# Second adjacency product, written out by step: three raw weight buffers, halves made one or two steps ahead, weights turned two steps later

## The chip, the cores and the metric

One core of a Trainium2 chip runs the whole program. The metric is the device time of one execution in microseconds, the median of several runs. TensorE is called PE here, VectorE DVE, ScalarE ACT, GpSimd POOL, SyncE SP.

## The reference, cut to what matters

Inputs: x (2048 x 512), adj (2048 x 2048), the weights of one shared and eight routed experts, a router, gamma and beta. All is float32.

```python
S = adj + adj.T, plus the identity, scaled on both sides by 1/sqrt(degree)
x = x + (adj @ S) @ layernorm(x)
h = layernorm(layernorm(x)) * gamma + beta
# _bit_quant: each row of a weight matrix becomes -1, 0 or +1 times the row's mean of abs
shared = silu(h @ q(w1s).T) @ q(w2s).T
routed = top-1 of 8 experts: gate * silu(h @ q(w1e).T) @ q(w2e).T
out = x + shared + routed
```

The kernel computes the graph term as two products: z = S u (first adjacency product), then y = adj z (second adjacency product). The change is about the second one and the work that runs beside it.

## The kernel before

**Stages.** To about 100 us adj and its transpose are streamed in and the first product is begun; to 198 us the first product is finished for the other columns while 28 weight chunks are quantised ("early rounds"). From 198 to 391 us the second product runs, 48 steps of it, with 36 more weight chunks beside it. From 391 us on the feed-forward tiles run, first the shared expert's, with the last 8 chunks beside them, then the routed ones.

**One step of the second product** (`macro` on each engine, four steps to a macro; J counts steps from 0 to 47). The 2048 output rows are done in groups of 6, 6 and 4 tiles of 128 rows (`Y_GROUPS`), each with its own PSUM banks `acc[k]` and 16 steps, one for each 128 rows of adj_t. In a step SP loads a strip of adj_t (`load_at`, 128 x 768 or 128 x 512 float32, two buffers, three in the last group), ACT makes its high float16 half (`high`, L924), DVE the low half (`low`, L1331), and PE does three matmuls of 512 columns for each bank: high by high, high by low, low by high (`parts`, L1622 to L1624). A step has 18 matmuls in the first two groups and 12 in the last. There are two buffers of halves, three in the last group.

**One weight chunk** (128 x 1024, q counts them; chunk 28 is the first of this stage; one a step except in steps 32 to 35 and from step 40 on). SP loads it (`load_w`, L489 and L492, two raw buffers), ACT sums its absolute values (`sums`, L871), DVE scales it to a byte (`ternary`, L1232 to L1259), PE transposes four blocks (`turn_w`, L1652), and ACT takes the sign back into SBUF (`store_w`, L885) three steps after its sums. Before PE turns chunk q, chunk q-2 must have been stored (`wt_ok`). Some early chunks are turned by a DMA on SP's queue (`turn`, L469), among them 25 and 27, and stored by L881.

**Between the groups** DVE adds x to the finished banks (`x1_of_group`, L1359), ACT issues the stores of these rows (`store_x1`, L961), and rows already there are normalised in pairs of tiles: part one and part two on DVE (`norm_parts`, L1303 to L1309 and L1314 to L1318), between them a power on POOL (L718), afterwards the halves of h on ACT (`h_high`, L955) and POOL (L725), and their store by POOL (L729). ACT waits for the stores of group 0 at step 20 and of group 1 at step 36 (`x1_stored`), before anything else of that step.

Each engine takes its instructions in the written order; across engines only semaphores order them. In a step ACT's order is high of J, store of chunk J-3, sums of chunk J, h_high; DVE's is low of J, ternary of J, normalising; PE's is turning the chunk of the step before, then the matmuls of J. On SP the load of adj_t for J comes before the load of the weights for J, and the first waits until the low half of J-2 has been made.

```python
pe.wait_ge(wt_ok, q - 1)                 # turn_w: chunk q-2 has been stored
pe.wait_ge(atlo_ok, STEPS * m + s + 1)   # macro on PE: the low half of this step
dve.wait_ge(p2_step, NT * (g + 1))       # x1_of_group: all banks of the group are done
```

## Time and profile before

| | us |
|---|---|
| median of 3 runs (669.05 to 671.61) | 669.19 |
| the profiled execution, its own time | 671.48 |
| its span, first to last instruction | 669.9 |
| PE busy | 616.7 (92%) |
| DVE busy | 481.1 (72%) |
| ACT busy | 373.1 (56%) |
| POOL busy | 179.0 (27%) |
| second product, first to last matmul | 198.2 to 391.1 |

Busy PE time is modelled for the end of each matmul; records of neighbours overlap, so the step from one start to the next says more than the duration. A "q" behind an engine's name is its sequencer: it issues DMAs and counts as no busy time. Idle time in square brackets stands before the instruction, with what ended it.

### The profile page before, as it was taken

The page shows a single profiled execution, that of the slowest core. Times are in us where ns is not written, and L with a number is a line of the kernel's source. Part 1 is how long each engine was busy: PE and PEld are TensorE (multiplying, and loading weights), DVE is VectorE, ACT ScalarE, POOL GpSimd, SP SyncE. Part 2 cuts the span into 40 slices and gives each one's busy share as a digit, 9 for nine tenths or more (in the row PEclk, how much of TensorE's full clock was granted, in tenths as well). Part 3 has the DMA queues.
Part 4 walks back from the last instruction along what each step waited for, and adds up shares of the span by engine and source line. Part 5 has one row for each costly group of instructions (what it writes and reads, how often), then busy time and mean ns, then how long its engine had stood idle before and what let it go on. Part 6 is the DMA issues. An engine that isn't in the chain of part 4 may idle for free.

```text
span 669.9 us, 14592 instructions
## 1 busy us (share of the span) xinstructions
PE 616.7 (92%) x4713; PEld 348.7 (52%) x4713; DVE 481.1 (72%) x1075; ACT 373.1 (56%) x699; POOL 179.0 (27%) x208
## 2 busy tenths in 40 slices
PE   0789899999999899999988999999999999999994
PEld 0334344444443444444433467776766676676762
DVE  4878986777775555677888659877885567666664
ACT  1667756677986777678756423556643334333241
POOL 2234343222210000003222406100120454444432
PEclk9999999999999899999999999999999999999999
DMA  8999990895878778777767966987249587788742
GB/s 341 417 417 416 421 356 15 175 239 160 233 206 282 241 256 290 267 250 230 233 226 246 226 184 140 242 208 200 80 67 235 152 198 184 173 167 194 182 135 59
DMA packets 106655, 149.81 MB, mean 224 GB/s; under 512 B 64510, under 2 KB 64510, under 8 KB 102496
## 3 DMA queue, kind: packets, MB, share of 16 engines
q1 hardware_dynamic: 91280, 116.82, 58.6%
q0 software_dynamic: 6512, 20.07, 10.3%
q10 hardware_dynamic: 8800, 12.09, 6.1%
q8 instruction: 38, 0.62, 0.4%
q14 instruction: 25, 0.20, 0.1%
HBM read 117.73 MB, written 18.25 MB: 203 GB/s over the span
## 4 chain that ended last, share of the span: by engine, by line
PE 47%; issue 29%; DVE 10%; DMA 8%; POOL 3%; ACT 1%; POOLq 0%; DVEq 0%; SPq 0%; ACTq 0%
PE bank L1745 14%; PE bank L1773 13%; DMA region<-in_adj_t 6%; PE bank L1622 5%; PE bank L1624 5%; PE bank L1623 5%; PE bank L1788 2%; DVE region L1145 2%; PE bank L1802 1%; DMA hb<-h_scratch,zreg 1%; DVE region L1141 1%; POOL rb L718 1%; DVE work L1400 1%; POOL hb L725 1%; DMA work<-hb 1%
## 5 line engine op out<-in xcount | busy, mean ns | idle before, releaser
L1773 PE MATMUL bank<-region,work 128*128 128x512 f16 (+1 forms) x512 | 116.9, 379 | 3.7 <-DVE work L1410 3.4
L1622 PE MATMUL bank<-zreg,work 128*128 (+1 forms) x256 | 97.7, 382 | 10.6 <-DVE work L1331 7.8
L1001 ACT ACTIVATE work<-work 128x512 f32<-128x512 f32 x64 | 39.8, 621 | 106.5 <-DVE work L1400 106.5
L1622 PE MATMUL bank<-region,work 128*128 128x512 f16 x192 | 74.0, 386 | 26.1 <-DVE region L1169 26.1
L1623 PE MATMUL bank<-zreg,work 128*128 (+1 forms) x256 | 97.5, 381 | 0.0
L1624 PE MATMUL bank<-zreg,work 128*128 (+1 forms) x256 | 97.5, 381 | 0.0
L871 ACT ACTIVATE junk<-work 128x512 f16<-128x512 f32 x116 | 72.8, 627 | 26.9 <-DMA work<-in_w 19.4
L1773 PEld LDWEIGHTS bank<-region,work 128*128 128x128 f16 x512 | 46.6, 98 | 61.6 <-issue 9.1
L1745 PE MATMUL bank<-zreg,region 128*128 128x128 f16 x1280 | 75.7, 219 | 0.0
L1745 PEld LDWEIGHTS bank<-zreg,region 128*128 128x128 f16 (+1 forms) x1280 | 72.7, 98 | 3.7
L1623 PE MATMUL bank<-region,work 128*128 128x512 f16 x192 | 74.0, 385 | 0.0
L1624 PE MATMUL bank<-region,work 128*128 128x512 f16 x192 | 73.8, 384 | 0.0
L1410 DVE SCALAR_TENSOR_TENSOR work<-work 128x512 f16<-128x512 f32 x64 | 43.6, 689 | 29.3 <-ACT work L1008 28.3
L1400 DVE TENSOR_TENSOR work<-bank,s 128x512 f32<-128x512 f32 x64 | 41.2, 685 | 25.7 <-PE bank L1745 24.6
L924 ACT ACTIVATE work<-work 128x768 f16<-128x768 f32 (+1 forms) x46 | 35.2, 764 | 38.9 <-PE bank L1624 21.2
L1259 DVE TENSOR_SCALAR work<-work,thr 128x512 int8<-128x512 f32 (+1 forms) x82 | 49.5, 634 | 4.1
L1331 DVE SCALAR_TENSOR_TENSOR work<-work 128x768 f16<-128x768 f32 (+1 forms) x48 | 42.6, 892 | 11.1 <-ACT work L924 10.9
L885 ACT ACTIVATE region<-bank 128x1024 f16<-128x1024 int8 (+1 forms) x44 | 44.3, 1007 | 6.8 <-DVE region L1359 6.8
L1745 PE MATMUL bank<-work,region 128*128 128x128 f16 x768 | 46.4, 220 | 1.1 <-DMA work<-hb 1.1
L1622 PEld LDWEIGHTS bank<-zreg,work 128*128 128x128 f16 x256 | 25.1, 98 | 41.4 <-DVE work L1331 8.5
L1745 PEld LDWEIGHTS bank<-work,region 128*128 (+1 forms) x768 | 43.6, 98 | 4.6 <-issue 2.0
L1622 PEld LDWEIGHTS bank<-region,work 128*128 128x128 f16 x192 | 19.0, 99 | 51.7 <-issue 20.7
(198 smaller groups left out, 1010.8 us busy)
## 6 DMA issues: line engine op xcount, KB each, us to landing
work<-in_w SPq DMA_DIRECT2D x58, 512.0 KB, 4.2
region<-in_adj SPq DMA_DIRECT2D x16, 1024.0 KB, 10.7
region<-in_adj_t SPq DMA_DIRECT2D x16, 1024.0 KB, 7.5
work<-in_adj_t SPq DMA_DIRECT2D x32, 384.0 KB, 4.4
xb<-in_w SPq DMA_DIRECT2D x10, 512.0 KB, 4.2
zreg<-s_scratch SPq DMA_DIRECT2D x17, 256.0 KB, 3.9
zreg<-in_x SPq DMA_DIRECT2D x4, 1024.0 KB, 9.8
h_scratch<-hb POOLq DMA_DIRECT2D x16, 256.0 KB, 4.4
```

Of the source, the lines that this page charges most:

```text
L871: nc.scalar.activation(junk[:, :], src[:, a * D:(a + 1) * D], ACT.Abs, accum_out=asum[:, b, a:a + 1]).then_inc(abs_ok, 1)
L885: nc.scalar.activation(values, pst8[turn_bank(q, b)], ACT.Sign).then_inc(wt_ok, 1)
L1001: nc.scalar.activation(h1[:, cols], pre[:, cols], ACT.Silu).then_inc(h1_ok, 1)
L1259: ins = nc.vector.tensor_scalar(bytes_, rows, thr[:, b, 0, a:a + 1], None, ALU.mult)
L1331: nc.vector.scalar_tensor_tensor(out=dst[:, 1, :], in0=src, scalar=A_SCALE, in1=dst[:, 0, :], op0=ALU.mult, op1=ALU.subtract).then_inc(atl ...
L1400: nc.vector.tensor_tensor(pre[:, half * 512:(half + 1) * 512].rearrange("p (f t) -> p f t", f=4), ps_h[b][half][:, :].rearrange("p (f t) - ...
L1410: nc.vector.scalar_tensor_tensor(out=h1hl[:, b, 1, cols], in0=h1[:, cols], scalar=U_SCALE, in1=h1hl[:, b, 0, cols], op0=ALU.mult, op1=ALU. ...
L1622: nc.tensor.matmul(dst, a_hi, b_hi, start=start, stop=False, skip_group_check=True)
L1623: nc.tensor.matmul(dst, a_hi, b_lo, start=False, stop=False, skip_group_check=True)
L1624: return nc.tensor.matmul(dst, a_lo, b_hi, start=False, stop=False, skip_group_check=True)
L1745: last = nc.tensor.matmul(ps_h[b][f // 4][:, (f % 4) * P:(f % 4 + 1) * P], w, ht[n % RING][:, c:c + P], start=(f % 4 == 0 and d == 0 and h ...
L1773: last = nc.tensor.matmul(ps_y[b][:, :].rearrange("p (d c) -> p d c", d=DB), h1hl[:, b, h, f * P:(f + 1) * P], w, start=(f == 0 and h == 0 ...
```

## The change

The stage is written out for all 48 steps instead of in loops of four, and its order is changed:

- Raw weights have three buffers instead of two. The load of chunk q waits for the quantising of chunk q-3 instead of q-2, and stands one step earlier in SP's queue.
- Halves have three buffers (four in the last group). In step J ACT and DVE make the halves of step J+1, in the last group those of J+2.
- PE turns the chunk of step J-2 in step J, instead of that of J-1.
- In the last step of a group each bank counts `y_acc`, and DVE evicts it singly, instead of all once the step is over. In step 32 DVE evicts four banks, makes a low half, and evicts the other two.
- The stores of the scales (`store_s2`) and of the rows of the first two groups (`store_x1`) move from ACT's queue to POOL's; those of group 1 stand there behind the third pair of tiles (t = 4) and ahead of the fourth (t = 6).
- The evictions that finish z (`z_high(2)`, `z_low(2)`) stand before the last early chunk instead of behind it.

The functions that go are in the listing above; here is the core of what comes.

```diff
--- before.py
+++ after.py
...
+RAW_RING = 3
...
         raw = work[:, 6144:6144 + 4096].bitcast(F32).rearrange("p (b n) -> p b n", b=2)
+        raw_more = w2t[:, 8 * CHUNK:10 * CHUNK].bitcast(F32)
+        hl_more = w2t[:, 10 * CHUNK:11 * CHUNK]
+        low_more = w2t[:, 7 * CHUNK:7 * CHUNK + HL]
...
+        def chunk_of(J):
+            if 0 <= J < 2 * NT:
+                return J
+            i = J - STEPS
+            return i if 2 * NT <= i < LATE_FROM - EARLY_CHUNKS else None
+        def raw_at(i):
+            return raw[:, i % RAW_RING, :] if i % RAW_RING < 2 else raw_more
+        def at_tile(J):
+            return at_end[:, J % NT % 3, :] if J >= 2 * NT else at[:, J % 2, 0:HL]
+        def at_landed(J):
+            if J >= 2 * NT:
+                return at_end_loaded[J % NT % 3], 16 * (J % NT // 3) + 16
+            return at_loaded[J % 2], 16 * (J // 2) + 16
+        def at_read(J):
+            if J >= 2 * NT + 3:
+                return J - 2
+            return min(J, 2 * NT + 1) - 1 if J <= 2 * NT else 2 * NT
+        def halves_at(J):
+            if J >= 2 * NT:
+                r = (J % NT + 3) % 4
+                return [hl_end[:, r, h, :] if r < 3 else hl_more[:, h * MH:(h + 1) * MH] for h in range(2)]
+            r = J % 3
+            return [hl[:, r, 0, :], hl[:, r, 1, :]] if r < 2 else [hl_more[:, 0:HL], low_more[:, :]]
+        def steps_before_halves(J):
+            k = J - 2 * NT
+            if k >= 4:
+                return J - 3
+            return (2 * NT - 2, 2 * NT - 1, 2 * NT, 2 * NT)[k] if k >= 0 else J - 2
+        def ahead_at(J):
+            if J < 2 * NT:
+                return [J + 1] if J >= 2 else [2] if J == 0 else []
+            return [n for n in ((J + 1, J + 2) if J == 2 * NT else (J + 2,)) if n < 3 * NT]
...
+            def load_w(i):
+                q, kind, c = later(i)
+                sp.wait_ge(tern_ok, q - 2)
+                if i == 2:
+                    sp.wait_ge(z_acc, NT)
...
+            def load_at(J):
+                g, j = divmod(J, NT)
+                c0, nc_ = Y_GROUPS[g][0] * P, Y_GROUPS[g][1] * P
+                if J >= 2:
+                    sp.wait_ge(atlo_ok, at_read(J))
+                sp.dma_start(at_tile(J), adjt_j[j, :, c0:c0 + nc_]).then_inc(at_landed(J)[0], 16)
...
+            load_w(0)
+            def y_step(J):
+                if chunk_of(J + 1) is not None:
+                    load_w(chunk_of(J + 1))
+                if J + 2 < 3 * NT:
+                    load_at(J + 2)
+                if J < 2:
+                    turn(EARLY_CHUNKS - 3 + 2 * J)
+                if J < NT and J % STEPS == STEPS - 1:
+                    t = 3 * (J // STEPS)
+                    if t == 0:
                         sp.wait_ge(z_acc, NT)
-                    sp.dma_start(xg_r[:, ds(3 * m, 3), :], x_t[:, ds(3 * m, 3), :]).then_inc(xg_in, 16)
+                    sp.dma_start(xg_r[:, t:t + 3, :], x_t[:, t:t + 3, :]).then_inc(xg_in, 16)
+                if J in (2 * NT + 9, 2 * NT + 10):
+                    load_last_x(J - 2 * NT - 9)
+                elif 2 * NT + 11 <= J <= 2 * NT + 14:
+                    load_shared(J - 2 * NT - 11)
...
+            def store_x1(g):
+                t0, count = Y_GROUPS[g]
+                for k in range(t0, t0 + count, 2):
+                    pool_wait(x1_ok, k + 2)
+                    pool.dma_start(x1_t[:, k:k + 2, :], xg_r[:, k:k + 2, :]).then_inc(x1_stored, 16)
+            store_s2(0, EARLY0, CHUNKS, S2_FROM[0])
+            store_s2(1, 0, 4, S2_FROM[1])
+            store_x1(0)
...
-            with pool.Fori(0, Y_GROUPS[2][0] // 2) as i:
+            with pool.Fori(0, Y_GROUPS[1][0] // 2) as i:
+                norm_pair(2 * i, pair=i)
+            store_x1(1)
+            with pool.Fori(Y_GROUPS[1][0] // 2, Y_GROUPS[2][0] // 2) as i:
                 norm_pair(2 * i, pair=i)
             norm_pair(12, True)
...
+                    if q == EARLY_CHUNKS - 1:
+                        z_high(2)
...
+            def high(J):
+                act.wait_ge(*at_landed(J))
+                if J >= 3:
+                    act.wait_ge(p2_step, steps_before_halves(J))
+                nc.scalar.activation(halves_at(J)[0], at_tile(J), ACT.Copy, scale=A_SCALE).then_inc(athi_ok, 1)
+            def y_step(J, norm_t=None):
+                for n in ahead_at(J):
+                    high(n)
+                if J == 1:
+                    store_w(early_at(EARLY_CHUNKS - 2), EARLY_CHUNKS % 2)
+                elif J == 3:
+                    store_w(early_at(EARLY_CHUNKS - 1), (EARLY_CHUNKS - 1) % 2)
+                i = chunk_of(J - LAG)
+                if i is not None:
+                    store_w(later(i), i % 2)
+                i = chunk_of(J)
+                if i is not None:
+                    act.wait_ge(raw_loaded[i % RAW_RING], 16 * (i // RAW_RING) + 16)
+                    sums(later(i), i % 2, raw_at(i))
+                if norm_t is not None:
+                    for e in range(2):
+                        h_high(norm_t + e, e)
...
-            z_high(2)
             store_w(early(ROUNDS - 1, early_count(ROUNDS - 1) - LAG), (EARLY_CHUNKS - LAG) % 2)
...
+            H_STEPS = {6 * STEPS: 0, 7 * STEPS: 2, 8 * STEPS: 4, 9 * STEPS + 1: 6, 10 * STEPS + 1: 8, 11 * STEPS + 1: 10}
+            for J in range(3 * NT):
+                if J == 5 * STEPS:
+                    act.wait_ge(x1_stored, 48)
+                elif J == 9 * STEPS:
+                    act.wait_ge(x1_stored, 96)
+                y_step(J, H_STEPS.get(J))
...
-                    if rnd == ROUNDS - 1 and s >= ROUND_STEPS - 2:
-                        low(0, s - ROUND_STEPS + 2, s % 2)
+                    if rnd == ROUNDS - 1 and s == ROUND_STEPS - 2:
+                        low(0)
+                    elif rnd == ROUNDS - 1 and s == ROUND_STEPS - 1:
+                        z_low(2, (0, 1))
+                        low(1)
+                        z_low(2, (2, 3))
...
+            NORM_STEPS = {STEPS * m + p * (1 if m == 7 else 2): (p, 2 * m - 10)
+                          for m in range(5, MACROS - 1) for p in range(2)}
+            def y_step(J):
+                ahead = ahead_at(J)
+                if J == NT:
+                    low(ahead[0])
+                    x1_of_group(0, xg_r[:, 0:6, :], range(6))
+                elif J == 2 * NT:
+                    low(ahead[0])
+                    x1_of_group(1, xg_r[:, 6:12, :], range(4))
+                    low(ahead[1])
+                    x1_of_group(1, xg_r[:, 6:12, :], range(4, 6))
+                else:
+                    for n in ahead:
+                        low(n)
+                i = chunk_of(J)
+                if i is not None:
+                    ternary(later(i), i % 2, raw_at(i))
+                if J in NORM_STEPS:
+                    norm_parts(*NORM_STEPS[J])
...
-                dve.wait_ge(p2_step, NT * (g + 1))
-                for k in range(count):
+                for k in ks:
+                    if k < count - 1:
+                        dve.wait_ge(y_acc, (Y_GROUPS[0][1] - 1) * g + k + 1)
+                    else:
+                        dve.wait_ge(p2_step, NT * (g + 1))
...
+            def y_step(J):
+                g, j = divmod(J, NT)
+                i = chunk_of(J - 2)
+                if i is not None:
+                    turn_w(later(i), i)
+                pe.wait_ge(atlo_ok, J + 1)
+                for k in (2, 3, 4, 5, 0, 1) if J == 0 else range(count):
+                    if J == 0:
+                        pe.wait_ge(zlo_ok, Z_LAST[k])
+                    elif j == 0:
+                        pe.wait_ge(x1_ok, Y_GROUPS[g - 1][0] + k + 1)
+                    last = parts(acc[k], *[v[:, k * P:(k + 1) * P] for v in halves_at(J)], z_hi[:, j, :], z_lo[:, j, :], j == 0)
+                    if j == NT - 1 and k < count - 1:
+                        last.then_inc(y_acc, 1)
+                last.then_inc(p2_step, 1)
+            for J in range(3 * NT):
+                y_step(J)
```

Where the order moves, by engine. First SP's queue at the start of the stage (work<-in_w are raw weights, work<-in_adj_t strips of adj_t; the transposes are chunks 25 and 27). Before, from the last early load on:

```order
L483 DMA xb<-in_w 128x1024
L469 DMA_TRANSPOSE region<-work 128x4x128
L489 DMA work<-in_w 128x2x512
L469 DMA_TRANSPOSE region<-work 128x4x128
L489 DMA work<-in_w 128x2x512
L497 DMA work<-in_adj_t 128x768
L489 DMA work<-in_w 128x2x512
L497 DMA work<-in_adj_t 128x768
L492 DMA work<-in_w 128x1024
L530 DMA region<-in_x 128x3x512
```

With the change:

```order
L533 DMA xb<-in_w 128x1024
L541 DMA work<-in_w 128x2x512 x2
L552 DMA work<-in_adj_t 128x768
L519 DMA_TRANSPOSE region<-work 128x4x128
L541 DMA region<-in_w 128x2x512
L552 DMA work<-in_adj_t 128x768
L519 DMA_TRANSPOSE region<-work 128x4x128
L544 DMA work<-in_w 128x1024
L552 DMA work<-in_adj_t 128x768
```

The transposes of chunks 25 and 27 stood ahead of the weights of steps 0 and 1; now they stand behind two and three loads.

ACT over the same place (L860 and L929 evict z; L871 and L940 sum; L881, L885 and L950, L954 store a chunk; L924 and L987 make high halves). Before:

```order
L871 ACTIVATE junk,asum<-work 128x512 x2
L885 ACTIVATE region<-bank 128x1024
L871 ACTIVATE junk,asum<-xb 128x512 x2
L860 ACTIVATE zreg<-bank,dinvz 128x512 x4
L881 ACTIVATE region<-region 128x1024
L871 ACTIVATE junk,asum<-work 128x512 x2
L885 ACTIVATE region<-bank 128x1024
L871 ACTIVATE junk,asum<-work 128x512 x2
L924 ACTIVATE work<-work 128x768
L881 ACTIVATE region<-region 128x1024
```

With the change:

```order
L940 ACTIVATE junk,asum<-work 128x512 x2
L929 ACTIVATE zreg<-bank,dinvz 128x512 x4
L954 ACTIVATE region<-bank 128x1024
L940 ACTIVATE junk,asum<-xb 128x512 x2
L950 ACTIVATE region<-region 128x1024
L987 ACTIVATE region<-work 128x768
L940 ACTIVATE junk,asum<-work 128x512 x2
L954 ACTIVATE region<-bank 128x1024
L940 ACTIVATE junk,asum<-work 128x512 x2
L987 ACTIVATE work<-work 128x768
L940 ACTIVATE junk,asum<-region 128x512 x2
L987 ACTIVATE work<-work 128x768
```

z is evicted one chunk earlier. The store of chunk 25 (the first L950 behind the evictions) stands ahead of the first high half, and the store of chunk 27 (the last L950) behind the high half of step 4.

POOL around the end of the third pair of tiles (rb<-rb,power is the power between the two parts of the normalising, h_scratch<-hb the stores of h). Before, one loop over all six pairs:

```order
L732 UNCONDITIONAL_BRANCH
L732 ISA
L718 TENSOR_TENSOR rb<-rb,power 128x2
L724 ISA
L725 TENSOR_TENSOR hb<-xb,hb 128x512
L724 REGISTER_ALU
L725 TENSOR_TENSOR hb<-xb,hb 128x512
L729 ISA
L729 DMA h_scratch<-hb 128x1024
L729 ISA
L729 DMA h_scratch<-hb 128x1024
L732 REGISTER_ALU
```

With the change:

```order
L795 DMA h_scratch<-hb 128x1024
L795 ISA
L795 DMA h_scratch<-hb 128x1024
L798 REGISTER_ALU
L798 COMPARE_AND_BRANCH
L774 DMA x_scratch<-region 128x2x512 x3
L801 UNCONDITIONAL_BRANCH
L801 ISA
L784 TENSOR_TENSOR rb<-rb,power 128x2
L790 ISA
```

The three stores of group 1 (x_scratch) stand behind the third pair and ahead of the power of the fourth, where no other engine's queue held them back before. The stores of scales and of group 0 stand ahead of the first pair in the same way.

## Rows read from the trace of the kernel before

**Rows 1.** PE's waits by window; waiter, awaited, us in total, times, longest; 196 to 268

```profile
PE bank L1652 <- ACT region L885: 2.8, 1, 2.8
PE bank L1622 <- DVE zreg L1219: 1.2, 1, 1.2
PE bank L1652 <- DVE work L1259: 1.1, 1, 1.1
```

**Rows 2.** the same view, 268 to 343.5

```profile
PE bank L1622 <- DVE work L1331: 2.2, 4, 0.8
PE bank L1622 <- DVE region L1359: 1.4, 2, 0.7
```

**Rows 3.** the same view, 343.5 to 391

```profile
PE bank L1622 <- DVE work L1331: 5.6, 6, 1.5
```

**Rows 4.** timeline of PE: start, us, what [idle before]; step 3 and the turn after it

```profile
213.41 0.38 PE L1622 MATMUL bank<-zreg,work 128*128 128x512 f16 x1
...
217.08 0.38 PE L1624 MATMUL bank<-zreg,work 128*128 128x512 f16 x1
220.28 0.61 PE L1652 MATMUL bank<-ident,work 128*128 128x128 f16 x4 [2.81 <-ACT region L885]
```

**Rows 5.** stages: stretch, us, PE busy (count), granted clock, DMA share, GB/s

```profile
220.00:223.00 3.00, 2.73 (x10) 0.50 0.49 126
```

**Rows 6.** timeline of ACT at the start of the stage

```profile
198.56 2.40 ACT L860 ACTIVATE zreg<-bank,dinvz 128x512 f16<-128x512 f32 x4
...
218.47 0.84 ACT L924 ACTIVATE work<-work 128x768 f16<-128x768 f32 x1 [5.05 <-PE bank L1624]
```

**Rows 7.** timeline of SP's queue at the start of the stage

```profile
197.89 0.38 SPq L489 DMA_DIRECT2D work<-in_w  x1
```

**Rows 8.** landing of SP's DMA transposes (L469)

```profile
DMA to landing us min/median/max: 2.4/3.0/5.0
```

**Rows 9.** landing of the strips of adj_t (L497), 195 to 340

```profile
DMA to landing us min/median/max: 2.5/4.3/7.0
```

**Rows 10.** landing of the stores of x1 (L961)

```profile
DMA to landing us min/median/max: 2.8/3.5/5.6
```

**Rows 11.** timeline of ACT around step 32 and later

```profile
342.45 2.76 ACTq L961 DMA_DIRECT2D x_scratch<-region  x3
...
350.45 0.63 ACT L924 ACTIVATE work<-work 128x512 f16<-128x512 f32 x1 [2.21 <-DMA x_scratch<-region]
...
364.81 0.63 ACT L871 ACTIVATE junk<-work 128x512 f16<-128x512 f32 x1 [2.79 <-DMA work<-in_w]
...
366.19 0.61 ACT L924 ACTIVATE work<-work 128x512 f16<-128x512 f32 x1
366.71 1.00 ACT L885 ACTIVATE region<-bank 128x1024 f16<-128x1024 int8 x1
```

**Rows 12.** timeline of DVE, from the eviction of group 1 on

```profile
341.13 3.68 DVE L1359 SCALAR_TENSOR_TENSOR region<-bank,region 128x512 f32<-128x512 f32 x6 [1.58 <-PE bank L1624]
...
345.33 1.27 DVE L1303 BATCH_NORM_STATS2 stb<-region 128x6 f32<-128x512 f32 x2
...
347.05 0.68 DVE L1331 SCALAR_TENSOR_TENSOR work<-work 128x512 f16<-128x512 f32 x1
...
361.15 0.16 DVE L1236 TENSOR_SCALAR s<-asum 128x2 f32<-128x2 f32 x1
...
362.41 1.41 DVE L1314 SCALAR_TENSOR_TENSOR xb<-region,mvb,gb 128x512 f32<-128x512 f32 x2
...
365.06 0.68 DVE L1331 SCALAR_TENSOR_TENSOR work<-work 128x512 f16<-128x512 f32 x1
```

**Rows 13.** timeline of POOL, 339 to 348

```profile
339.32 2.37 POOL L725 TENSOR_TENSOR hb<-xb,hb 128x512 f16<-128x512 f32 x2 [10.31 <-ACT hb L955]
341.63 0.58 POOL L729 DMA_DIRECT2D h_scratch<-hb  x1
...
347.23 1.08 POOL L718 TENSOR_TENSOR rb<-rb,power 128x2 f32<-128x2 f32 x1 [4.27 <-DVE rb L1309]
```

228 lines of the change are left out of this document (48 added, 180 removed).

## Prediction

> **What bounds the kernel now.** The engine shares come first: PE is busy for 92% of the span, so the end moves by what PE gains or loses. Then the waits of PE alone, by stretches of the stage that is changed. At its start PE idles 5.1 us in three waits [rows 1]: for the evicted z, for a quantised chunk, and for 2.8 us for a chunk that ACT had not stored. In the middle, up to the eviction of group 1, it idles 3.6 us in six waits [rows 2], in the last group 5.6 us in six [rows 3]. The timeline of one step shows what a wait really costs: 17 starts take 217.08 - 213.41 = 3.67 us, so 0.216 us each; the next start was due at 217.30 and came at 220.28 [rows 4]. That is 2.98 us for an idle time of 2.81, because the record of a matmul is 0.16 longer than its pitch. So each wait costs its idle time and 0.16. Behind the long one the granted clock is 0.50 (1.2 GHz instead of 2.4) in a stretch of 3 us [rows 5]: 2.7 us of busy time at half speed, 1.35 us lost. In all: start 5.1 + 0.5 + 1.35 = 7.0, middle 3.6 + 1.0 = 4.6, last group 5.6 + 1.0 = 6.6; together **18.2 us**. More this change can't get: matmuls and transposes stay the same in number. Behind the stage everything starts from its last matmul, so I carry its gain to the end one to one.
>
> **Start of the stage.** Evicting z one chunk earlier lets ACT begin at about 196.3 instead of 198.56 [rows 6], and the wait for z shrinks from 1.4 us to some 0.2. But the queues behind it get worse. Two weights have to be stored before PE may turn chunks 28 and 29, and both come late:
>
> - Chunk 28. The transpose of chunk 25 now stands behind the load of weights that is free at 197.89 [rows 7] and a strip of adj_t, with an issue of 0.4 us each: it goes at 198.7. Transposes landed after 2.4 to 5.0 us [rows 8]; I take 4.4, near the upper end, because 896 KB go ahead of it in its queue: 203.1. ACT then stores chunk 25 (1.00), makes the high half of step 2 (0.84) and sums chunk 28 (366.19 - 364.81 = 1.38), and DVE quantises it (362.41 - 361.15 = 1.26) [rows 6, 11, 12]: 207.6, with hand-overs 207.8. PE gets there after two steps of 18 x 0.216 from 198.2, at 206.2 with its turns. It waits 1.6 us (0 with the fastest landing, 2.2 with the slowest).
> - Chunk 29. Its turn asks for chunk 27 to be stored, and on ACT that stands behind the high half of step 4, whose strip stands on SP behind a load that waits until chunk 28 is quantised. From there 0.4 + 4.3 (2.5 to 7.0) [rows 9] + 0.84 + 1.00 = 6.5 us, while PE has 4.1 us of work. It waits 2.4 us (0.6 to 5.1).
>
> The clock may fall again: after idles of 1.2 and 1.1 us it didn't, after 2.8 it did. The second wait is nearest to the latter, so I take one fall, 1.35 us (none to two for the range). The wait on ACT for the stores of the scales (L969), behind which ACT idled 5.05 us and then stood ahead of PE [rows 6], is gone: those stores go to POOL, which has nothing else then. What is late next is just what is listed. Sum: 0.2 + 1.6 + 2.4 + 1.35 = 5.6 against 7.0: **1.4 us gained**.
>
> **Middle.** Halves made a step ahead take away the four waits for a low half: DVE was late there because part two of the normalising, 365.06 - 362.41 = 2.65 us [rows 12], stood ahead of it, and a lead of a step, 3.9 us, covers that. Banks evicted singly take away both waits for an eviction: four of six banks are out before the step ends. Load of weights one step ahead and the third buffer cost no engine anything; the turn two steps behind needs no more buffers than there are (four quantised slots). I count the whole 4.6 us as **gained**, with 0.5 for what may be left.
>
> **Last group.** Here a lead of two steps (5.2 us) meets a new delay. ACT still waits at step 36 until group 1 is stored, and these stores now stand on POOL behind the third pair. Count from B, the end of step 31 (341.1 before, where DVE begins to evict [rows 12]). Before, they were issued by 345.2 and ACT was free at 350.45 = B + 9.3, after 5.2 us of landing [rows 11]. Now ACT makes the high half of step 34 (0.5), stores a chunk (0.9) and makes one half of h (0.6): B + 2.0. POOL makes the low halves (2.4) and issues two stores of h (0.58 each and 0.2 between): B + 5.7 [rows 13]. Then come the three stores. No row shows POOL issuing 512 KB; the nearest are 256 KB in 0.58 us. Bounds are that and its double; I take 0.8 and 0.2 between: B + 8.7. For landing I take 5.6, the slowest of those issued by ACT (2.8 to 5.6 [rows 10]), since two stores of h are ahead in the same queue: **B + 14.3** (11.5 to 15.3). The Trainium skill's page DMA: Bandwidth & Descriptors (Anatomy of one DMA) gives about 2.0 us and bytes over 436 GB/s for a DMA issued from GpSimd: 3.2 us here, an estimate. By it they would land at B + 11.9 and the next wait of PE would vanish, 2.2 us less; the 5.2 us of rows 11 speak against it.
>
> From there step by step:
>
> - Chunk 60 must be turned in step 38. High half 0.5, sums 1.4, quantising 1.3 and hand-overs: B + 17.7. PE needs six steps of 12 x 0.216 = 2.59: B + 15.5. It waits 2.2 us (0 to 3.2).
> - Chunk 61: between two quantisings DVE has part one (347.05 - 345.33 = 1.7) and a low half (0.6), so 1.26 + 1.7 + 0.6 = 3.6 against PE's 2.8: 0.8 us.
> - Chunk 62 asks for chunk 60 stored, behind the high half of step 41. Its strip waits on SP behind a load of weights that waits for chunk 60's quantising. Some 5.1 to landing, 0.5 + 1.4 + 0.5 + 0.9 of ACT: 8.4, against 3.6 + 2.8: 2.0 us.
> - Chunk 63: quantising of chunk 62 at 8.3, part two 2.65, a low half 0.6, 1.26: 12.8, against 8.4 + 2.8: 1.6 us.
>
> Sum 6.6, just what is lost now: **nothing gained**. With no hold on ACT only the last, 1.6, stays; with the upper bound of the landing (3.2 instead of 2.2) and a strip 0.9 later it is 8.5: +5.0 to -1.9. Only because PE waits here are the low halves on time in steps 40 to 47.
>
> **POOL and DVE.** POOL's power for the fourth pair comes behind the three stores: B + 8.7 + 1.1 = 9.8 [rows 13]. DVE's part two waits for it, and behind that stands the low half of step 37: 9.8 + 2.65 + 0.6 = B + 13.1. PE wants it at 5 x 2.59 = B + 13.0. It costs 0.1, but there is no room left.
>
> **Sum.** 1.4 + 4.6 + 0 = 6.0 us. The profiled execution took 671.48, so 665.5; it lies 2.3 us above the median of 669.19, for which the trace gives no reason, and on the median's footing the forecast is **663.2 us**. Each part of the program outside the stage is unchanged; loops written out add rows only.
>
> **Rivals.** A measurement of this kernel tells a change of about 0.5%, 3.35 us, from none.
>
> 1. *As above*, gain 3.4 to 9 us, 660.2 to 665.8: 0.55. For it: the waits follow from the order of SP's and ACT's queues, whatever the exact landings.
> 2. *The waits at the end of the stage go too.* If group 1 lands by about B + 11.5, ACT is not held and the lead of two steps swallows the rest but 1.6 us: 1.4 + 4.6 + 5.0 = 11 us, 658.2; without the waits at the start (4.0) 654.2. For it: 3.5 us is the median of landings [rows 10]. The skill's rule above leads here as well. Against it: DMA engines are full around the boundary. 0.17.
> 3. *No gain.* Strips land late: chunk 29 waits 3.9 instead of 2.4, chunk 28 waits 2.2, the clock falls twice, the last group loses 8.5. Start 0.2 + 2.2 + 3.9 + 2.7 = 9.0, so -2.0 + 4.6 - 1.9 = +0.7: 668.5. For it: rows 9 reach 7.0. 0.22.
> 4. *Slower: POOL becomes the gate at the boundary.* If a store of 512 KB holds POOL for longer than taken, each us of it delays the fourth power, the low half of step 37 and the landing by 3 us. It eats the gain of 6.0 at 0.8 + 2.0 us a store and gives a slowdown of over 3.35 from 0.8 + 3.1: at 4.0 us a store 672.8. Against it: 0.58 for 256 KB. 0.06.
>
> The range that leaves out no more than 2 in 10 runs from 657 (most of rival 2 with the waits at the start kept) to 668 (most of rival 3). Faster by over 0.5% are cases 1 and 2: 0.72; same 0.22; slower 0.06.
>
> **What would show it.** Right: PE waits of 1 to 3 us at the turns behind steps 1 and 2 (near 206 and 211), none from 215 until the boundary, none for a low half at the group ends; ACT's longest idle there, 8 us or more, ends with a store of x1 landing; then four waits of PE at turns in steps 38 to 41, for DVE and ACT. The stage ends 6 us earlier than 391.1. Wrong: PE waits for low halves in the last group, or a turn never waits; POOL issues an x1 store in over 2 us; the stages behind take another time than before.

## The result, and the profile after

The changed kernel takes **665.7 us** where the kernel before takes 671.0 in the same series (medians of 19 runs each). The ratio is 0.9927, 95% interval 0.9913 to 0.9942: 5.3 us, 0.7% faster. The forecast was 6.0 us, 663.2 on a median of 669.2. The profiled span went from 669.9 to 663.7 us. From the first to the last start of a matmul of the second adjacency product it was 192.5 us and is 187.4. What lies around the stage took 477.3 and 476.2.

PE's waits in the changed kernel, in the stretches of [rows 1], [rows 2] and [rows 3] (here 196 to 219, 219 to 343, 343.5 to 386; the second has no row, PE waits for nothing there):

```profile
PE bank L1708 <- ACT region L950: 2.2, 1, 2.2
PE bank L1708 <- DVE work L1308: 2.1, 2, 1.8
...
PE bank L1708 <- DVE work L1308: 5.4, 3, 3.5
```

L1708 is the turn of a chunk, L1308 its quantising on DVE, L950 the store of chunk 27 on ACT. Not one wait is for a low half or an eviction any more: PE waits only at turns. Its timeline has the five longer ones with their times (chunks 28, 29, 60, 61 and 63; the sixth, 0.3 us for chunk 26 at 197.8, is not shown):

```profile
207.79 0.40 PE L1708 MATMUL bank<-ident,work 128*128 128x128 f16 x4 [1.78 <-DVE work L1308]
214.32 0.38 PE L1708 MATMUL bank<-ident,work 128*128 128x128 f16 x4 [2.24 <-ACT region L950]
...
354.75 0.61 PE L1708 MATMUL bank<-ident,work 128*128 128x128 f16 x4 [3.45 <-DVE work L1308]
355.15 0.63 PE L1678 MATMUL bank<-zreg,work 128*128 128x512 f16 x1
355.57 0.63 PE L1679 MATMUL bank<-zreg,work 128*128 128x512 f16 x1
...
359.84 0.34 PE L1708 MATMUL bank<-ident,work 128*128 128x128 f16 x3 [0.44 <-DVE work L1308]
...
367.34 0.40 PE L1708 MATMUL bank<-ident,work 128*128 128x128 f16 x4 [1.52 <-DVE work L1308]
```

From 354.75 a matmul takes 0.63 us and the next starts 0.42 later, not 0.38 and 0.216 as in [rows 4]: a second fall of the clock, which the forecast did not have. The stages view (stretch, us, busy time and count of PE, PEld, DVE, ACT, POOL, granted clock, DMA share, GB/s) has it too, above the rest of the stage:

```profile
196.00:219.00 23.00, 18.64 (x86) 7.86 (x85) 14.91 (x44) 18.80 (x39) 0.00 (x0) 0.93 0.80 264
219.00:268.00 49.00, 49.00 (x264) 23.72 (x263) 28.93 (x77) 36.82 (x73) 3.62 (x7) 1.00 0.84 276
268.00:343.50 75.50, 75.50 (x405) 36.39 (x403) 58.64 (x142) 55.35 (x106) 19.43 (x24) 1.00 0.73 244
343.50:386.00 42.50, 37.07 (x179) 16.63 (x177) 27.34 (x57) 19.44 (x38) 12.90 (x15) 0.96 0.77 227
...
354.00:358.00 4.00, 3.25 (x11) 1.46 (x12) 3.90 (x9) 2.19 (x6) 2.22 (x2) 0.59 0.56 164
```

To compare kernels I take each start of PE in the stage and subtract the pitch at which it should follow the one before (0.216 us for a product, 0.058 for a quarter of a turn); what is over 0.15 us counts as lost, the clock's falls with it. The turn just ahead of the stage (chunk 26) is counted with its start.

| lost on PE, us | forecast: before, after | measured: before | measured: after |
|---|---|---|---|
| start of the stage | 7.0, 5.6 | 7.5 | 6.5 |
| middle | 4.6, 0 | 4.8 | 0 |
| last group | 6.6, 6.6 | 6.5 | 7.7 |
| sum | 18.2, 12.2 | 18.8 | 14.2 |

What PE's long wait at 354.75 hangs on is seen on POOL and ACT. Step 31, the last of group 1, ends at 335.4 here, so that is B, the point from which the prediction counts. POOL's timeline, then the end of ACT's hold:

```profile
337.55 2.27 POOL L791 TENSOR_TENSOR hb<-xb,hb 128x512 f16<-128x512 f32 x2 [14.11 <-ACT hb L1012]
339.76 0.58 POOL L795 DMA_DIRECT2D h_scratch<-hb  x1
340.55 0.54 POOL L795 DMA_DIRECT2D h_scratch<-hb  x1 [0.21 <-issue]
341.25 2.19 POOL L774 DMA_DIRECT2D x_scratch<-region  x3 [0.16 <-issue]
343.46 0.72 POOL L784 TENSOR_TENSOR rb<-rb,power 128x2 f32<-128x2 f32 x1
```

```profile
351.30 0.63 ACT L987 ACTIVATE work<-work 128x512 f16<-128x512 f32 x1 [9.64 <-PE bank L1680]
```

ACT idles for 9.6 us. The view names PE, whose step had long been done; the third experiment shows that it is the stores. The trace has it as well: the last store was issued at 342.7 and landed 8.6 us later, at 351.3, where ACT goes on. The view of L774, the line that stores x1, has its durations in ns and the landing:

```profile
L774 POOL DMA_DIRECT2D x_scratch<-region x6: 727/736/835, 269.2 to 342.7; - x6
...
DMA to landing us min/median/max: 4.0/7.3/8.6
```

### The profile page after: what moved, and what is told of

Read it like the earlier page. It is cut to its first block, busy times and chain, and to the rows that moved or that the text cites. A ratio compares the mean times of both kernels' runs of the same rounds, so it can differ in the third digit from the quotient of the medians.

```text
span 663.7 us, 14071 instructions
## 1 busy us (share of the span) xinstructions
PE 615.6 (93%) x4713; PEld 348.9 (53%) x4713; DVE 478.0 (72%) x1075; ACT 371.7 (56%) x699; POOL 185.8 (28%) x222
## 4 chain that ended last, share of the span: by engine, by line
PE 64%; DMA 13%; DVE 12%; issue 5%; ACT 4%; SPq 1%; POOL 1%; DVEq 0%; ACTq 0%; POOLq 0%
PE bank L1785 14%; PE bank L1813 13%; PE bank L1680 10%; PE bank L1678 10%; PE bank L1679 10%; DMA region<-in_adj_t 7%; DMA work<-in_w 3%; PE bank L1828 2%; ACT junk L940 2%; DVE region L1194 2%; PE bank L1842 1%; DMA hb<-h_scratch,zreg 1%; PE bank L1708 1%; DVE region L1190 1%; DVE work L1308 1%
## 5 line engine op out<-in xcount | busy, mean ns | idle before, releaser
L1678 PE MATMUL bank<-zreg,work 128*128 128x512 f16 x180 | 69.6, 386 | 0.0
L1680 PE MATMUL bank<-zreg,work 128*128 128x512 f16 x180 | 69.5, 386 | 0.0
L1679 PE MATMUL bank<-zreg,work 128*128 128x512 f16 x180 | 69.5, 386 | 0.0
L940 ACT ACTIVATE junk<-work 128x512 f16<-128x512 f32 x92 | 57.6, 626 | 13.8 <-DMA work<-in_w 9.0
L987 ACT ACTIVATE work<-work 128x768 f16<-128x768 f32 (+1 forms) x32 | 24.3, 760 | 36.4 <-PE bank L1680 25.9
L954 ACT ACTIVATE region<-bank 128x1024 f16<-128x1024 int8 x44 | 44.3, 1007 | 0.0
L1057 ACT ACTIVATE work<-work 128x512 f16<-128x512 f32 x64 | 40.3, 630 | 6.1 <-ACT work L1049 0.4
L849 POOL DMA_INDIRECT out<-zreg x23 | 23.4, 1019 | 66.2 <-DVE zreg L1499 32.4
L712 POOL TENSOR_TENSOR dv<-dv,power 128x1 f32<-128x1 f32 x16 | 21.1, 1322 | 61.1 <-DVE dv L1202 61.1
```

The costliest lines, as they stand in the source:

```text
L940: nc.scalar.activation(junk[:, :], src[:, a * D:(a + 1) * D], ACT.Abs, accum_out=asum[:, b, a:a + 1]).then_inc(abs_ok, 1)
L954: nc.scalar.activation(values, pst8[turn_bank(q, b)], ACT.Sign).then_inc(wt_ok, 1)
L987: nc.scalar.activation(halves_at(J)[0], at_tile(J), ACT.Copy, scale=A_SCALE).then_inc(athi_ok, 1)
L1057: nc.scalar.activation(h1hl[:, b, 0, cols], h1[:, cols], ACT.Copy, scale=U_SCALE).then_inc(h1hi_ok, 1)
L1678: nc.tensor.matmul(dst, a_hi, b_hi, start=start, stop=False, skip_group_check=True)
L1679: nc.tensor.matmul(dst, a_hi, b_lo, start=False, stop=False, skip_group_check=True)
```

## The experiments

Each ratio is to the kernel before in the same series: 668.5 or 668.9 us for the experiments, 671.0 for the changed kernel's first row. The medians are of 2 runs in experiment 10 and of 4 to 10 in the others. The stage column is the length from the first to the last start of a matmul of the stage in the profiled run; what lies around it, untouched by any of these edits, took 474.6 to 478.6 us, so single runs differ there by 4 us that mean nothing, and the stage is the finer measure.

| kernel | median us | ratio to before (95%) | stage us | lost on PE us |
|---|---|---|---|---|
| before | 671.0, 668.5, 668.9 | 1 | 192.5 | 18.8 |
| changed | 665.7 | 0.9927 (0.9913 to 0.9942) | 187.4 | 14.2 |
| 1: transposes ahead of loads | 663.9 | 0.9928 (0.9906 to 0.9950) | 186.9 | 13.0 |
| 2: chunk 27 stored first | 660.7 | 0.9878 (0.9853 to 0.9902) | 183.8 | 10.2 |
| 3: ACT's hold at the end | 660.7 | 0.9882 (0.9858 to 0.9905) | 183.3 | 10.1 |
| 4: all three | 656.9 | 0.9834 (0.9808 to 0.9861) | 178.9 | 5.3 |
| 5: changed, again | 664.3 | 0.9937 (0.9915 to 0.9958) | 186.2 | 12.5 |
| 6: no lead in the queue | 662.1 | 0.9918 (0.9888 to 0.9948) | 185.6 | 11.6 |
| 7: evicted at once | 666.1 | 0.9959 (0.9939 to 0.9978) | 188.6 | 14.7 |
| 8: before, loops written out | 666.7 | 0.9975 (0.9954 to 0.9996) | 189.7 | 15.6 |
| 9: 8, evicted singly | 666.3 | 0.9961 (0.9939 to 0.9982) | 188.2 | 14.6 |
| 10: waits as with two raw buffers | 705.4 | 1.0549 (1.0506 to 1.0593) | 227.5 | 53 |
| 11: turned one step behind | 672.9 | 1.0052 (1.0029 to 1.0074) | 196.4 | 22.5 |
| 12: all three and more | 658.2 | 0.9839 (0.9798 to 0.9881) | 178.7 | 4.9 |

### The start of the stage and the hold (1 to 4)

**Experiment 1.** SP issues both DMA transposes ahead of the loads.

```diff
+            turn(EARLY_CHUNKS - 3)
             load_w(0)
             def y_step(J):
+                if J == 1:
+                    turn(EARLY_CHUNKS - 1)
                 if chunk_of(J + 1) is not None:
                     load_w(chunk_of(J + 1))
                 if J + 2 < 3 * NT:
                     load_at(J + 2)
-                if J < 2:
-                    turn(EARLY_CHUNKS - 3 + 2 * J)
```

> The changed kernel with one edit on SP's queue: the transposes of chunks 25 and 27 stand ahead of the loads of steps 0 and 1 again. My theory: PE's wait at the first turn (1.78 us idle in the changed kernel) comes from the transpose of chunk 25 landing behind two loads. ACT then stores chunk 25 straight after its sums, and the strip of step 2 (about 4.3 us behind 198.3) becomes what is late: the wait shrinks to 0.3 us or so, the second wait (2.24) stays. Time 1.5 us under the changed kernel's 665.7: 664.2 on the footing of before at 671. Rival: ACT and DVE are late by themselves there, because the eviction of z now stands ahead of the last early chunk; then the wait stays at 1.5 us or more and the time is unchanged.

The wait for chunk 28 shrinks from 1.8 to 0.6 us, but the one for chunk 29 behind it grows from 2.2 to 2.9. PE's waits, 196 to 219:

```profile
PE bank L1709 <- ACT region L951: 2.9, 1, 2.9
PE bank L1709 <- DVE work L1309: 0.6, 1, 0.6
```

Expected were 1.5 us less. Lost on PE are 13.0 us; the changed kernel lost 14.2 in its first profile and 12.5 in its second (experiment 5), so no gain is shown, and the ratio can't be told from the changed kernel's either. A wait on a chain of steps is partly handed on to the next one.

**Experiment 2.** On ACT the store of chunk 27 goes ahead of the high half of step 4.

```diff
             def y_step(J, norm_t=None):
+                if J == 3:
+                    store_w(early_at(EARLY_CHUNKS - 1), (EARLY_CHUNKS - 1) % 2)
                 for n in ahead_at(J):
                     high(n)
...
-                elif J == 3:
-                    store_w(early_at(EARLY_CHUNKS - 1), (EARLY_CHUNKS - 1) % 2)
```

> The changed kernel with one edit on ACT: in step 3 chunk 27 is stored ahead of the high half of step 4, not behind it. My theory: PE's second wait (2.24 us idle, for ACT's store) is the strip of step 4 landing, which has nothing to do with chunk 27. The wait goes, and with it the fall of the clock behind it (8 matmuls at half speed, 1.6 us): 4.0 us faster, 661.7. Rival 1: the wait moves on to the next turn (chunk 30 asks for chunk 28 stored, which stays behind the same high half), then PE waits 1 us or more a step later. Rival 2: the fall of the clock does not depend on this wait (the first one, 1.78 us, is enough); then 1.6 us less is gained, 663.3.

One wait is left at the start (1.7 us, chunk 28), and with the long one the clock's fall is gone. The rows are PE's waits from 196 to 219, and the stage from 212 on:

```profile
PE bank L1708 <- DVE work L1308: 1.7, 1, 1.7
```

```profile
212.00:219.00 7.00, 7.00 (x37) 3.32 (x36) 4.49 (x16) 6.06 (x12) 0.46 (x1) 1.00 0.99 341
```

So it is the place on ACT's queue that makes chunk 29 late, behind a strip that has nothing to do with it. The ratio is 0.49% of the time before under the changed kernel's, 3.3 us, and the stage 3.6 us shorter, where 4.0 were expected.

**Experiment 3.** ACT waits for the stores of group 1's x1 after step 47, not at step 36.

```diff
-                elif J == 9 * STEPS:
-                    act.wait_ge(x1_stored, 96)
                 y_step(J, H_STEPS.get(J))
+            act.wait_ge(x1_stored, 96)
             act.wait_ge(abs_ok, 2 * LATE_FROM)
```

> The changed kernel with ACT's wait for the stores of group 1 moved from step 36 to behind step 47 (nothing that these 12 steps write lies over those rows). My theory: ACT's hold of 9.6 us is what makes the quantising of chunk 60 late. PE's wait of 3.45 us and the one of 0.44 go with the fall of the clock behind them (1.6 us); the ones at chunks 62 and 63 stay at 1.5 us each, since they come from a strip behind a load on SP and from part two of the normalising. 4 us faster: 661.7. Rival: POOL's power for the fourth pair (DVE idles 3.2 us for it) is the gate, since the low halves stand behind it; then PE still waits 2 us or more in steps 37 to 39 and the time falls by less than 2 us.

ACT's idle of 9.64 us is gone; its timeline there, and PE's waits from 343 to the end of the stage:

```profile
341.53 0.63 ACT L987 ACTIVATE work<-work 128x512 f16<-128x512 f32 x1 [0.19 <-PE bank L1679]
346.07 0.63 ACT L987 ACTIVATE work<-work 128x512 f16<-128x512 f32 x1 [3.90 <-DMA work<-in_adj_t]
...
348.97 0.63 ACT L987 ACTIVATE work<-work 128x512 f16<-128x512 f32 x1 [0.91 <-DMA work<-in_adj_t]
```

```profile
PE bank L1707 <- DVE work L1307: 2.1, 2, 1.5
PE bank L1707 <- ACT region L954: 0.4, 1, 0.4
```

The last group loses 3.0 us instead of 7.7. Chunk 60's wait falls from 3.45 to 0.58 us, the clock stays up, and chunk 63's 1.52 stays. So the hold behind the stores of x1 is what cost the last group its gain: 4.7 us by the starts in one profile, where the prediction had 5.0 for it. The stage as a whole is 4.1 us shorter, since its start happened to lose more than in the changed kernel's profile.

**Experiment 4.** The three edits together.

> The three edits together. My theory: the waits are independent of each other, so the gains add up: 1.5 + 4.0 + 4.0 = 9.5 us under the changed kernel, 656 us, 0.979 of before; PE idles at most 4 us in the whole stage and its clock never falls there. Rival: once these waits are gone the DMA engines or DVE set the pace, and the sum comes to 6 us or less (660).

656.9 us; 12 us under the kernel before, and PE's longest wait is 1.5 us. The clock doesn't fall in the stage. The median is the lowest of the study. Expected were 9.5 us under the changed kernel: by the ratios it is 6.2 to 6.9 us and by the stage 7.3 to 8.5 (against its two measurements). So the gains did not add up in full; chunk 29 still waits 1.3 us here.

### The middle (5 to 9)

**Experiment 5.** The changed kernel again, to have it beside the next three.

> The changed kernel once more, beside the three others of this call, so that they can be set against it on one chip. Expected: 0.992 to 0.993 of the time before, and the same waits of PE as in its first profile, within 0.5 us each (chunk 28 1.8, chunk 29 2.2, chunk 60 3.4, chunk 63 1.5), nothing in the middle.

The ratio agrees. The single waits do not repeat: chunk 28 waited 2.5 us and chunk 29 0.7 (3.2 together; 4.0 in the first profile), chunk 61 2.1 instead of 0.4. Only their sums may be compared between kernels, and those to 1 or 2 us: all that PE lost is 12.5 us here and 14.2 in the first profile.

**Experiment 6.** The halves of step J + 1 are made at the end of step J, where the kernel before had them in its queues; the third buffer and the late turn stay.

```diff
+                if not 2 <= J < 2 * NT - 1:
                     for n in ahead_at(J):
                         high(n)
...
+                if 2 <= J < 2 * NT - 1:
+                    high(J + 1)
```

> The halves of steps 3 to 31 are made at the end of the step before instead of at its beginning, so on ACT and DVE they stand behind the sums, the stores, the quantising and the normalising again, in the order in which the kernel before had them; the third buffer of halves and the turn two steps behind stay (only the eviction of group 0 keeps its order). By the prediction (the lead in the queue covers part two of the normalising, 2.65 us) the four waits for a low half in the middle come back: PE idles some 2 us more between 220 and 340 us, and chunk 29, whose store now stands ahead of the high half of step 4, waits less: about 0 to 2 us slower than the changed kernel less 2 us, so 0 in the sum. By the rival (it is the third buffer and the later turn that cured the middle, since they let a half be made while PE still reads the two before) the middle stays without a wait, and the start gains 2.5 us: 0.988 to 0.989 of the time before.

The same edit stands on DVE for low, save at J = 16. The middle stays without a wait for a low half. Its one new wait is for the eviction of group 0 (1.0 us: DVE's low half of step 17 stands ahead of the evictions and now waits for a high half that ACT makes later). The start of the stage loses 2.3 us instead of 5.1 (experiment 5) or 6.5 (first profile), since chunk 29 no longer waits. So the lead is not needed for the middle. The intervals of experiments 5 and 6 overlap.

**Experiment 7.** All banks of a group evicted after its last step.

```diff
-                    if k < count - 1:
-                        dve.wait_ge(y_acc, (Y_GROUPS[0][1] - 1) * g + k + 1)
-                    else:
-                        dve.wait_ge(p2_step, NT * (g + 1))
+                    dve.wait_ge(p2_step, NT * (g + 1))
```

> All banks of a group are evicted after its last step again, instead of singly as each has its last product; all else is the changed kernel. By the prediction PE then idles at both boundaries of groups again, 0.7 us each and 0.16: 1.7 us more in the middle. But what comes behind the second boundary hangs on ACT, not on DVE or PE: x1 of group 1 is stored about 1 us later, while PE too comes 0.8 us later to the turn of chunk 60, so little more is lost there (0 to 1 us). Sum 1.0 to 2.7 us slower than the changed kernel. If the evictions are on no path: the same time.

Both waits come back as in [rows 2]:

```profile
PE bank L1675 <- DVE region L1417: 1.4, 2, 0.7
```

The stage is 2.4 us longer than in experiment 5 and 1.2 longer than in the first profile; the medians lie 1.8 us apart. So single evictions are worth about what was counted.

**Experiment 8.** The kernel before, each loop over blocks of four steps unrolled.

```diff
-                with pe.Fori(m0 + 1, m0 + NT // STEPS) as m:
+                for m in range(m0 + 1, m0 + NT // STEPS):
```

> The kernel before with its loops over blocks of four steps written out and nothing else changed: same instructions, same waits, same order. If loops on the engines cost nothing on the path: 1.000 (0.997 to 1.003) of the time before, with the same waits of PE (2.8 us for chunk 27 at 217, six waits in the middle, 3.6 us). If a part of the gain came from writing the steps out (registers and branches at the loops' ends, where three of the waits in the middle lie), 1 to 2 us faster.

The same edit was made in all six loops of SP, ACT, DVE and PE. The time is 0.9975 of before, just outside no change, and the stage 2.9 us shorter. PE's waits for low halves between 219 and 340 shrink from 2.2 us in four [rows 2] to one:

```profile
PE bank L1622 <- DVE region L1359: 1.4, 2, 0.7
PE bank L1622 <- DVE work L1331: 0.2, 1, 0.2
```

Where the time goes is seen where one engine hands over to another. First ACT's last instruction of the sums and the first of DVE's quantising in the kernel before, inside a loop; then the same pair in experiment 8:

```profile
289.25 0.19 ACT L871 ACTIVATION_READ_ACCUMULATOR junk<-work 128x1 f32 x1
...
289.61 0.17 DVE L1236 TENSOR_SCALAR s<-asum 128x2 f32 x1 [1.47 <-ACT junk L871]
```

```profile
288.00 0.19 ACT L871 ACTIVATION_READ_ACCUMULATOR junk<-work 128x1 f32 x1
...
288.22 0.17 DVE L1236 TENSOR_SCALAR s<-asum 128x2 f32<-128x2 f32 x1 [1.31 <-ACT junk L871]
```

From the end of one to the start of the other it is 0.18 us in the loop (289.432 to 289.610) and 0.03 without it. But the wait itself is not what costs. In the same loop, for the same semaphore, a chunk of the other weight matrix has its sums taken over by L1232, and that hand-over takes 0.03 us:

```profile
249.54 0.19 ACT L871 ACTIVATION_READ_ACCUMULATOR junk<-work 128x1 f32 x1
...
249.76 0.21 DVE L1232 TENSOR_SCALAR thr<-asum 128x1 f32<-128x1 f32 x1 [1.32 <-ACT junk L871]
```

The difference is on DVE's sequencer. The view of L1236 in the kernel before has, beside DVE's own instructions, this row; in experiment 8 it has none:

```profile
L1236 DVEq FUSED_REGOPS  x16: 75/76/93, 229.2 to 331.7; - x16
```

Between 225 and 340 us all 13 such hand-overs to L1236 inside the loops take 0.16 to 0.19 us; those to L1232 (5) and from the high half to the low half (10), inside loops as well, take 0.03, and so do all of them in experiment 8. A second reckoning, of the number that a wait compares with, stands ahead of L1259 behind another wait: 0.13 us instead of 0.04. On SP the issue of a load starts 0.17 to 0.20 us after DVE's end in 38 of 47 cases, with such a row in between, and after 0.03 in the other nine; in experiment 8 after 0.03 in all 50. So in a step inside the loops two loads (0.14 each) and the quantising (0.13 and 0.09) start later than they need, 0.5 us of a step of 3.9. That this is what made the low halves late is worked out, not tried by itself; the branches at the loops' ends went with the same edit.

**Experiment 9.** Experiment 8 and the banks evicted singly.

```diff
+                        if STEPS * m + s == NT * (g + 1) - 1 and k < count - 1:
+                            last.then_inc(y_acc, 1)
```

> The kernel before with its loops written out and, besides, its banks evicted singly; one weight and one half at a time, two buffers and the order of the queues as before. If these two edits are what cures the middle, PE waits there for less than 0.5 us in all (18 waits and losses of the kernel before: 5.0 us by the starts, 2.3 with the loops written out alone), and the time is 1.0 to 1.7 us under that of the loops alone: 0.995 of the time before (0.993 to 0.997). If the third buffers and the lead of a step are needed, some 2 us of waits for low halves stay.

DVE's side is the one that experiment 7 takes away. From 225 to 340 us no wait of PE is left, as in the changed kernel; by the starts 0.3 us is lost. So two of the change's edits are enough for the gain in the middle, 4.5 of 4.8 us, with two buffers of halves, two raw buffers and no lead. The last group gives some of it back, as it does in the changed kernel: it loses 7.9 us (6.5 before), with a new wait of 2.6 and a fall of the clock behind it. Of the 6.3 or 5.1 us by which the changed kernel's stage is shorter, 4.4 are in experiment 9, and all other edits have 0.7 to 1.9 together.

### What the buffers and the late turn are worth (10, 11)

**Experiment 10.**

```diff
-                sp.wait_ge(tern_ok, q - 2)
+                sp.wait_ge(tern_ok, q - 1)
```

> The changed kernel, but each load of weights waits until the chunk before it is quantised, as it had to with two raw buffers (the third stays, unused in effect). The prediction called the third buffer free and gave it nothing. If the order on SP counts: the strip of step J + 2 stands behind the weights of chunk J + 1, so it is issued only when chunk J is quantised, and the next quantising hangs on that strip: 0.4 of issue, 4.3 of landing, 0.8 high half, 0.9 store, 1.4 sums, 1.3 quantising, about 5 to 9 us a step against PE's 3.9, so 20 to 100 us slower. If the third buffer is worth nothing: the time of the changed kernel, 0.993.

36.6 us slower than before. SP's queue, 240 to 262 us:

```profile
244.61 0.38 SPq L541 DMA_DIRECT2D work<-in_w  x1
245.04 1.17 SPq L552 DMA_DIRECT2D work<-in_adj_t  x1
247.94 0.37 SPq L541 DMA_DIRECT2D work<-in_w  x1
248.35 0.47 SPq L552 DMA_DIRECT2D work<-in_adj_t  x1
254.93 0.34 SPq L544 DMA_DIRECT2D region<-in_w  x1
```

Each strip goes out right behind the weights, so it hangs on a quantising it has nothing to do with, and the next quantising hangs on it: (254.93 - 244.61) / 2 = 5.2 us a step here, and 4.9 on the mean of ten loads from 224.9 to 273.5, where the changed kernel has 4.0 and PE 3.9 us of work. With halves made a step ahead the third raw buffer is needed, not for the weights but for what stands behind them on SP.

**Experiment 11.**

```diff
-                i = chunk_of(J - 2)
+                i = chunk_of(J - 1)
```

> The changed kernel, but PE turns a chunk one step behind its quantising instead of two, as the kernel before did. The quantising of chunk J - 1 ends only shortly before PE is through with step J - 1, since DVE is 70% busy; the prediction gave the later turn no price. If it is worth something, PE waits at the turns after every normalising part and at the start of the stage: 3 to 8 us slower than the changed kernel, 0.998 to 1.004 of the time before. If not: 0.993.

4.1 us slower than before, 8 to 9 slower than the changed kernel (expected 3 to 8). PE's waits from 195 to the end of the stage:

```profile
PE bank L1708 <- DVE work L1308: 10.6, 3, 5.5
PE bank L1708 <- ACT region L950: 2.0, 1, 2.0
PE bank L1708 <- ACT region L954: 1.8, 1, 1.8
```

The long ones (5.5, 2.0 and 4.2 us) stand where they stood, at chunks 28, 29 and 60, each with a step less of cover. The middle has none; the turn right behind it, at the start of the last group, waits 1.8. So the later turn is what makes the longer queues of the change bearable.

### A version that beats both (12)

> The three edits of the fourth experiment together (both transposes ahead of the loads, chunk 27 stored first, ACT's wait for x1 put to the end of the stage), the halves of steps 3 to 31 made at the end of the step before (save at the boundary of group 0), and part two of the normalising of the fifth pair put one step later, behind the quantising of chunk 63, for which PE waited 1.5 us. Fourth experiment 0.983 of the time before; chunk 63's wait gone 1.7 us, the two waits at the start smaller by 1 to 2 us: 0.978 to 0.981, with less than 2.5 us lost on PE in the whole stage.

```diff
-            NORM_STEPS = {STEPS * m + p * (1 if m == 7 else 2): (p, 2 * m - 10)
+            NORM_STEPS = {STEPS * m + p * (1 if m == 7 else 3 if m == 9 else 2): (p, 2 * m - 10)
```

Chunk 63's wait is gone as meant (0.2 us for a low half is left), but chunk 60 waits 1.5 us where it waited 0.3 in experiment 4:

```profile
350.13 1.78 DVE L1311 TENSOR_SCALAR work<-work,thr 128x512 int8<-128x512 f32 x2
```

```profile
350.22 2.70 POOL L792 TENSOR_TENSOR hb<-xb,hb 128x512 f16<-128x512 f32 x2 [9.72 <-ACT hb L1016]
```

The rows are DVE's quantising of chunk 60 and what POOL does then. The pair of instructions takes 1.78 us where it took 0.89 in experiment 4, since POOL makes the low half of h at the same time. But that is not what differs: in experiment 4 POOL held DVE up just ahead of the same quantising, by about as much (L1285, 1.12 us instead of 0.17). What differs is a strip. ACT's high half ahead of the sums of chunk 60, in experiment 4 and in this one:

```profile
343.32 0.63 ACT L988 ACTIVATE work<-work 128x512 f16<-128x512 f32 x1 [1.00 <-DMA work<-in_adj_t]
```

```profile
347.62 0.63 ACT L988 ACTIVATE work<-work 128x512 f16<-128x512 f32 x1 [3.15 <-DMA work<-in_adj_t]
```

The strip took 6.4 us to land in the one (issued at 336.87) and 9.1 in the other (338.48), so the sums come 3.4 us later, counted from the start of step 32. Whether the fifth edit has to do with that or it is chance, one profile can't tell. Expected were a ratio of 0.978 to 0.981 and less than 2.5 us lost; it is 0.984 and 4.9. The stage is as long as in experiment 4 (178.7 and 178.9), and the ratios can't be told apart. Both kernels beat the changed one by 0.9% of the time before, with intervals that don't touch its own; the three edits of experiment 4 are enough.

## Why the prediction was right, and where it was not

The direction, the size (5.3 us against 6.0) and the range hold. That the size came out so close is in part luck: the middle's gain is there for another reason than the one given, and it is by far the largest term. 5.3 us is 0.8% of the time before and the interval of the ratio excludes no change. Step by step:

- **Start.** Forecast: waits of 1.6 and 2.4 us for chunks 28 and 29, one fall of the clock. Measured: 1.8 and 2.2 and one fall, 1.6 us instead of 1.35; gained 1.0 instead of 1.4. The second profile has 2.5 and 0.7, so that the two came out so close is luck, and their sum is not (4.0 forecast, 4.0 and 3.2 measured). Experiments 1, 2 and 4 confirm the two causes: a transpose behind two loads on SP, a store behind a strip on ACT. The wait for z ended as forecast; in its place the first turn (chunk 26) waited 0.3.
- **Middle.** The gain was right (4.6 forecast, 4.8 measured), **and the reason for more than half of it was not the one that mattered**. The steps that failed are "a lead of a step, 3.9 us, covers that", and the one in the sum, "loops written out add rows only". With the lead taken away (experiment 6) the waits for low halves stay away; with nothing but the loops written out (experiment 8) they go from 2.2 us to 0.2. Part two of the normalising made the low halves late only together with what the loops cost (0.5 us a step, by the hand-overs). Whether the lead would have been enough with the loops kept was not tried. The part for the evictions (0.7 us each and 0.16) was right (experiments 7 and 9).
- **Last group.** Forecast 6.6 us, as before: measured 7.7 (before 6.5), so 1.2 more lost. The step that was off is the landing of x1, "I take 5.6, the slowest of those issued by ACT". Issued by POOL the last of them took 8.6 us from its start and 7.9 from the end of its issue. Issue was a little cheaper than taken (three stores done at B + 8.0, not B + 8.7; 0.73 us each, not 0.8 and a pause). ACT came free at B + 15.9, not B + 14.3. Chunk 60 waited 3.45 instead of 2.2, a little over the upper bound of 3.2. The clock fell behind it: 1.6 us that were not in the sum. Chunk 61 waited 0.4 and chunk 62 nothing, where 0.8 and 2.0 were forecast: what they need went on while PE waited for chunk 60. Chunk 63: 1.5 us, 1.6 forecast.
- **POOL and DVE.** The power for the fourth pair ended at B + 8.8 (9.8 forecast), and DVE's part two took it up at once. No low half was late there. POOL was no gate: rival 4 falls with 0.73 us a store.
- **Rival 2** was right on what the end hangs on and wrong on the landing. Experiment 3 gives what it forecast without the hold (4.7 of 5.0 us). The estimate of 3.2 us for the landing, by the Trainium skill's page DMA: Bandwidth & Descriptors (Anatomy of one DMA), lies below the fastest of the six, 4.0 us; the slowest took 8.6, with the DMA engines 84% busy while it was under way (342.7 to 351.3).
- **Rival 3**, no gain, needed both chunks at the start late and a clock that falls twice. The second fall came, but at the other end of the stage.
- What stands ahead of the prediction on the load of weights needs a correction. Against the strips its place on SP's queue is unchanged: the weights of chunk J + 1 went out ahead of the strip of step J + 2 before too. What changed is what it waits for, one quantising less. Experiment 10 shows that the other edits can't do without this.

## What to carry to other kernels

When a change rewrites a loop and moves work as well, run the unrolled old version alone: here it had 2.9 of the 5 to 6 us of the stage, and about a third of the gain by the medians. An engine that must wait for a transfer whose result nobody on that engine needs soon (ACT for the stores of x1, ACT for a strip ahead of a store that PE needs) is worth looking for first: with two such waits moved (and the transposes) the stage got 7.3 to 8.5 us shorter, where all edits of the change but the loops and the evictions brought 0.7 to 1.9 together. And a lead in one queue can need a buffer in another, because of what stands behind the load there.
